# Queries and keys of a later attention's first chunk, projected inside the MLP's last group

## The reference, cut to what matters

```python
def _layer(x, wqkv, qs, ksc, wo, lg, lb, w1, b1, w2, b2):
    h = shift_token(x)                      # second half of the columns comes from the token before
    q, k, v = jnp.split(h @ wqkv, 3, axis=-1)
    q = l2norm(to_heads(q)) * qs
    k = l2norm(to_heads(k)) * ksc
    q, k = rotary_xpos(q, k)
    o = local_attention(q, k, v)            # window of 128: each chunk sees itself and the one before
    x = x + o @ wo
    h = (shift_token(x) - mu) / jnp.sqrt(var + 1e-05) * lg + lb
    a, g = jnp.split(h @ w1 + b1, 2, axis=-1)
    return x + (a * jax.nn.gelu(g, approximate=False)) @ w2 + b2

x = _layernorm(x + block_A(x))
x = _layernorm(x + block_B_layers_0_and_1(x))
```

## Time and profile before

| | us |
|---|---|
| median of 3 runs | 1943.41 |
| lowest and highest | 1942.41, 1944.68 |
| the profiled execution, its own time | 1944.76 |
| its span, first to last instruction | 1943.0 |
| PE busy in the span | 1837.0 (95%) |
| DVE busy | 1585.9 (82%) |
| ACT busy | 1190.5 (61%) |
| POOL busy | 1086.3 (56%) |

### The profile page before, as it was taken

The page is one execution under the profiler, slowest core; times in us unless marked ns, Lnnn a source line. Parts: engine busy times, 40 slices in busy tenths (PEclk is TensorE's granted clock), DMA queues, the critical chain, the costliest instruction groups (busy, mean ns, idle before and its releaser), DMA issues.

```text
span 1943.0 us, 43269 instructions
## 1 busy us (share of the span) xinstructions
PE 1837.0 (95%) x15168; PEld 1540.9 (79%) x15168; DVE 1585.9 (82%) x3853; ACT 1190.5 (61%) x3084; POOL 1086.3 (56%) x1040
## 2 busy tenths in 40 slices
...
DMA packets 139667, 116.01 MB, mean 60 GB/s; under 512 B 10440, under 2 KB 138704, under 8 KB 138704
## 3 DMA queue, kind: packets, MB, share of 16 engines
...
## 4 chain that ended last, share of the span: by engine, by line
PE 63%; ACT 14%; DVE 11%; issue 7%; POOL 4%; DMA 0%; ACTq 0%; SPq 0%; DVEq 0%; POOLq 0%
PE psum L519 14%; PE psum L520 13%; PE psum L521 13%; PE psum L806 7%; ACT b_probs L1606 6%; PE psum L773 3%; PE psum L787 3%; DVE psum L1057 2%; PE psum L818 2%; PE psum L620 2%; ACT a_probs L1503 2%; ACT b_pt L1615 2%; DVE a_neg_max L1059 1%; PE psum L709 1%; ACT k_t_hi L1588 1%
## 5 line engine op out<-in xcount | busy, mean ns | idle before, releaser
L1606 ACT ACTIVATE b_probs<-masked,neg_max 128x256 f32<-128x256 f32 (+1 forms) x512 | 250.1, 499 | 3.5 <-DVE neg_max L1175 3.4
L519 PE MATMUL psum<-wa_hi,b_h_hi 128*128 128x512 f32 (+1 forms) x576 | 235.5, 409 | 3.9 <-DVE g_new L1346 2.4
L520 PE MATMUL psum<-wa_lo,b_h_hi 128*128 128x512 f32 (+1 forms) x576 | 215.5, 374 | 0.0
L521 PE MATMUL psum<-wa_hi,b_h_lo 128*128 128x512 f32 (+1 forms) x576 | 215.2, 374 | 0.0
L1175 DVE CUSTOM_DVE_ANT_0 masked<-psum,mask 128x256 f32<-128x256 f32 (+1 forms) x512 | 182.3, 412 | 39.1 <-PE psum L773 33.0
L519 PE MATMUL psum<-g_h_hi,wm_hi 128*128 128x512 f32 (+1 forms) x480 | 192.9, 402 | 11.5 <-POOL g_h_lo L1844 9.6
L520 PE MATMUL psum<-g_h_lo,wm_hi 128*128 128x512 f32 (+1 forms) x480 | 191.4, 399 | 0.0
L521 PE MATMUL psum<-g_h_hi,wm_lo 128*128 128x512 f32 (+1 forms) x480 | 191.2, 398 | 0.0
L1801 POOL TENSOR_TENSOR rnorm<-norm2c,minus_half 128x16 f32<-128x16 f32 x64 | 187.1, 2923 | 0.9 <-DVE norm2c L1135 0.9
L1686 ACT ACTIVATE gate<-psum,vec_b 128x512 f32<-128x512 f32 x96 | 66.0, 687 | 180.2 <-PE psum L521 180.1
L519 PE MATMUL psum<-wm_hi,u_hi 128*128 128x256 f32 x576 | 165.9, 288 | 0.1
...
## 6 DMA issues: line engine op xcount, KB each, us to landing
...
```

The lines of the kernel that those rows point to most:

```text
L519: nc.tensor.matmul(out, a_hi, b_hi, start=first, stop=False)
L520: nc.tensor.matmul(out, a_hi, b_lo, start=False, stop=False)
L521: return nc.tensor.matmul(out, a_lo, b_hi, start=False, stop=last)
L1606: ins = nc.scalar.activation(out, src, ACT.Exp, bias=neg_max[:, r, k:k + 1], scale=-1.0, accum_out=row_sum[:, n % 2, 4 * r + k:4 * r + k + 1])
```

## The change

**TensorE.** In the last group of MLP A and of MLP B of layer 0 the opening of the next attention is in two parts. `opening=1`, the transposes of chunks 0 and 1, moves to the group's start, into bank 4. `opening=2` is new: `project_q(0)` and `project_k(0)`, 12 matmuls, between the last tile of `hidden` and `down(t, 0)`, into banks 4 and 5. Behind `down(t, 1)` PE no longer waits for `y_added` before the first projection; the wait is at `project_k(1)`.

```diff
--- before.py
+++ after.py
@@
+        sbuf("b_space", [P, 1552], at=b_ctx)
+        squares = [sbuf("q_sq", [P, 2, 512], at=b_ctx), sbuf("k_sq", [P, 2, 512], at=b_ctx)]
+        g_in_flat = [t[:].rearrange("p c a d -> p (c a d)") for t in g_in]
+        cos_part = [g_in_flat[0][:, 512 * i:512 * i + 512] for i in range(2)]
+        rope = g_in_flat[0][:, 1024:1280].rearrange("p (a d) -> p a d", a=4)
+        norm2, norm2c, rnorm = [g_in_flat[0][:, 1280 + 16 * i:1296 + 16 * i] for i in range(3)]
+        rot = [g_in_flat[1][:, 512 * i:512 * i + 512] for i in range(2)]
@@ sp_attention, sp_mlp
-                if s == 2 * U + 8:
+                if s == NCH - 2:
...
+                if c is MLP_B:
+                    sp.wait_ge(SB["q_rot"], (layer + 1) * NCH)
+                    sp.wait_ge(SB["k_rot"], (layer + 1) * NCH)
                 load(0, 0)
...
+                if c is MLP_B:
+                    sp.wait_ge(SB["qk_t"], 2 * (layer + 1) * NCH)
                 load(1, 1)
@@ pe_attention
-                project(n, 0, W0)
+                project(n, 0, W0 if n else bank[4])
...
-                project(n, 1, W1)
+                project(n, 1, W1 if n else bank[5])
...
-            if opening:
+            if opening == 1:
                 transpose_x(0)
                 transpose_x(1)
+                return
+            if opening == 2:
+                project_q(0)
+                project_k(0)
                 return
@@ pe_mlp, group
+                if overlap:
+                    pe_attention(pe, next_layer(layer), opening=1)
                 for f in range(c.NF):
                     hidden(t, f, steady)
...
+                if overlap:
+                    pe_attention(pe, next_layer(layer), opening=2)
                 down(t, 0)
-                if not more and next_layer(layer) < LAYERS:
-                    pe_attention(pe, next_layer(layer), opening=True)
                 down(t, 1)
@@ dve_attention
+            if opening == 2:
+                norms(0, 1)
+                norms(0, 0)
+                rotate_q(0)
+                return
...
-                    if b_chunk(s + 1):
+                    if s == -1:
+                        scale_rotated(0)
+                        h_low(2)
+                        dve_mlp(v, *((MLP_A, MA, None) if layer == 0 else (MLP_B, MB, layer - 1)), opening="finish")
+                    elif b_chunk(s + 1):
                         rotate_q(s + 1)
@@ dve_mlp, group
+                    if f == 0 and overlap:
+                        dve_attention(v, next_layer(layer), opening=1)
+                    if f == 1 and overlap:
+                        finish_stats(t - 1, 1 - slot)
+                    if f == 3 and overlap:
+                        finish(t - 1, 1 - slot)
...
-                if not more and next_layer(layer) < LAYERS:
-                    dve_attention(v, next_layer(layer), opening=True)
+                if overlap:
+                    dve_attention(v, next_layer(layer), opening=2)
                 add_product(t, slot, 0)
@@ act_attention, act_mlp
+            if opening == 2:
+                if layer == 0:
+                    a.wait_ge(MA["fin_ready"], NGRP - 1)
+                else:
+                    a.wait_ge(MB["fin_ready"], layer * NGRP - 1)
+                copy_qk(0, 0)
+                copy_qk(0, 1)
                 return
@@ pool_attention, pool_mlp
+            if opening:
+                tables(0)
+                rotate_k(0)
+                inverse_norms(0)
+                return
...
+                if overlap:
+                    inverse_std_behind(t - 1)
...
+                if overlap:
+                    pool_attention(pool, next_layer(layer), opening=True)
```

82 lines of the change are left out of this document (39 added, 43 removed).

## The result

The changed kernel takes 1931.83 us (median of 5 runs, 1930.35 to 1936.03) where the kernel before took 1943.41 beside it. The ratio is 0.9943, with a 95% interval of 0.9927 to 0.9959: 11.1 us faster, 8.0 to 14.2 (the ratio is not that of the two medians, which are 11.6 us apart). The forecast was 15.1. The profiled execution is one of the slower ones: 1934.86 us, span 1933.1.

The account below looks back on a forecast made before the run. Attention B was taken as PE-bound, the handovers as waiting for rotated keys. Gains 39.1 - (2.8 + 17.3 + 11.1) = 7.9 and 39.9 - (2.8 + 17.6 + 11.1) = 8.4, together 16.3, 15.1 with one clock fall: 1928.3 us, range 1925.0 to 1932.0.

Parts of the forecast that it names:

- the handover up to chunk 1: From the MLP's old end to chunk 1's key transposes: 2.8 + 17.3 us at the first handover, 2.8 + 17.6 at the second.
- E': End of the MLP's last `down` matmul in the new order, predicted 2.8 us later than in the old order.
- The release by `k_sq`: Chunk 0's key transposes start at E' + 6.7, released by ACT's square after some 1.2 us of PE idle time.
- 17.3: Chunk 1's key transposes can start at E' + 17.3 at the first handover, 7.65 us behind the first scores.
- buffers and loads: New buffer places and the MLP's loads at s = 30 were taken to cost nothing.
- to the measuring point it took 11.1: From chunk 1's key transposes to chunk 2's, behind each handover: 11.1 us at full clock.
- "39.1" and "39.9": Old order's distances from the MLP's last matmul to chunk 2's key transposes, in us, at the first and second handover.
- I take one fall in two handovers: PE's granted clock falls behind chunk 1's wait at one of the two handovers, costing 1.2 us.
- The row against the lock: At the second handover DVE's `add_old` beside POOL's power costs nothing; blocking would have cost some 2.3 us.
- Less: Rival, 0.17: gain eaten behind first scores by POOL's slower chunk 1 chain or blocked `add_old`; gain 12.9 or 11.6 us.
- It does not do what it says: Rival, 0.07: DVE or POOL falls behind in the MLP's last group, 4 us lost per handover; 1936 us.
- slower: Rival, 0.03: rotation instructions slow down and DVE bounds the attention; at 1.5 us more per chunk, 1966 us.

Follow-up runs that it names:

- e1_memory: Old order at both handovers, with the change's new buffer places and its MLP input loads at s = 30; 1943.48 us, ratio 0.9998 to the kernel before.
- with the clock held: The change and the kernel before, each with extra matmuls in PE's waits over 0.6 us at the program's handovers; 1917.41 and 1928.00 us.
- e4_norms_quiet: The change with DVE's norms of chunks 1 and 2 early and POOL's rotation of chunk 1's keys behind the closing `finish`; 1931.82 us.

## Why the prediction was right and wrong

**Right: the handover up to chunk 1.** The 12 matmuls delay the last product by 2.8 us at the first handover and 2.5 at the second, from end to end (2.6 and 2.3 up to the start of the projection of v, as E' is read in the first trace). `down` follows them without a gap: DVE's extra work in the group cost nothing. This held although finish(t - 1) took 3.71 us in place of 1.38, beside POOL's residual; the slack of the earlier trace rows bore it. The release by `k_sq` at E' + 6.8 after 1.27 us of idle time, the first scores at E' + 9.55 and 9.8, chunk 1's transposes at E' + 17.6 and 17.85: none off by more than 0.3 us. The last of them is in part luck. The parts that the prediction names for 17.3 are 8.3 + 4.0 + 2.90 + 1.86 = 17.1, so 0.2 us have no source, and the power of chunk 1 took 3.36 us in place of 2.90 at both handovers. POOL's power of chunk 0 ended at 632.80, E' - 0.35 (predicted - 1.3), and at the second handover at E' + 3.9 (3.5), ahead of the statistics both times.

**Right: buffers and loads.** No cost of an address, no wait at the first `g_stats`, a period of 13.2 us: e1_memory measured 0.9998.

**Wrong: "to the measuring point it took 11.1".** This term was mis-sized; it measured 11.9 with the clock held (11.85 to 11.88 in six handovers). I took it from a row in which PE came late to chunk 1 itself, so that DVE's and POOL's chain of chunk 2 was ahead of it. In the new order PE waits for that chain at both chunks, so the distance is one whole round of it. I had named POOL's chain of chunk 1 as what is late next, and then let chunk 2 follow from a row where it was not late. This is 0.8 us per handover with the clock held, 0.36 for the lost start and 0.45 for a longer power.

**Wrong: "39.1" and "39.9" as the old order's own distance.** This is the larger error: the prediction took the clock's fall off the new order's gain, but not out of the old order's distances. They hold a fall each: 37.5 and 38.2 with the clock held. Without any fall the sum of the prediction would be 11.5 and not 16.3 us: 3.3 for these two and 1.6 for the term above make 11.4. In the kernels without extra matmuls the falls are there in both orders, and cost more in the old one (filling the waits took 16.8 us off it and 13 to 14 off the new one), so that 11 to 13 us come out.

**Mis-sized: the clock.** "I take one fall in two handovers" at 1.2 us. The first trace had one in both, at least 1.5 and 0.5 us by the difference to 11.88. And the larger part of the clock's luck in that trace was not in the handovers at all, but 4.6 us in attention A, which no term of mine had. Over the traces without extra matmuls in attention A that stretch varies from -1.2 to +4.6 us; the two medians of the change are 1.5 us apart.

**The row against the lock.** I had weighed DVE's sum beside POOL's power and taken no cost, which stands. The changed kernel has the very case at the second handover, POOL's power and DVE's `add_old`:

```profile
1283.79 2.91 POOL L1833 TENSOR_TENSOR g_in<-g_in,minus_half 128x16 f32<-128x16 f32 x1
```

```profile
1284.04 1.23 DVE L1367 TENSOR_TENSOR g_sum<-g_new,g_old 128x1024 f32<-128x1024 f32 x1
```

The sum takes 1.23 us inside the power, and 1.22 at the first handover, where POOL is idle. So it did not block, and the 2.3 us of that price were rightly left out. What I did not look for were POOL's instructions on 256 and 512 columns beside DVE: `g_fin` 3.17 against 1.37 (removed in e4_norms_quiet by keeping POOL away), and, by rows alone, 3.71 for finish(t - 1) beside POOL's residual (617.68 to 620.28) and `q_cos` of chunk 1 at 644.59 with 1.46 us against 0.68, while POOL's sum ran from 644.22 to 645.50. The Trainium skill ("SBUF — State Buffer", Who interferes with whom) says that `tensor_scalar` in a two-port mode and GpSimd lock each other out for a whole instruction, and that a two-input `tensor_tensor` in SBUF contends with a GpSimd instruction that reads SBUF. These rows agree with both. Which mode `g_fin` ran in no run here shows. The power on 16 columns, by the earlier trace rows and the two rows above, is the case in which no blocking showed, though the page makes no exception for it.

**The rivals.** "Less" came nearest: a gain of 11.6 to 12.9 against 11.1 and 13.4, but by the clock and the term of 11.9; POOL's slower power of chunk 1 gave only 0.46 us at each handover, where the rival had 1.1, and `add_old` did not block. "It does not do what it says" and "slower" are out.
